# Output projection of the last four token tiles as three fp32r products, with half of W2 loaded later

## The reference, cut to what matters

```python
x = x + xattn(layernorm(x), ctx_1024, ...)   # 16 heads of 64; ends with: out @ Wo + bo, out is [1024, 1024], Wo is [1024, 256]
x = x + linear_attn(layernorm(x), ...)       # 16 heads of 16, causal within 64 tokens
x = x + ffn(layernorm(x), ...)               # top 2 of 8 experts; h = relu(x @ W1[e] + b1[e]); h @ W2[e] + b2[e]
```

## Time and profile before

| | |
|---|---|
| median of 3 runs | 1303.89 us (1302.39 to 1304.11) |
| profiled execution | 1302.54 us, span 1300.8 us |
| PE busy | 1272.9 us, 98% of the span |
| DVE, ACT, GpSimd busy | 75%, 47%, 47% |
| DMA, all queues | 145.56 MB, mean 112 GB/s |
| share of PE in the chain that ended last | 94% |

### The profile page before, as it was taken

How to read it: one execution, slowest core, us unless ns; L and a number is a source line. 1 busy time by engine, 2 the same in 40 slices (tenths; PEclk the granted TensorE clock), 3 DMA queues, 4 the chain that set the end, 5 groups by cost and what they waited for, 6 DMA issues and landing times.

```text
span 1300.8 us, 43872 instructions
## 1 busy us (share of the span) xinstructions
PE 1272.9 (98%) x18276; PEld 1135.4 (87%) x18276; DVE 979.4 (75%) x1970; ACT 616.1 (47%) x1250; POOL 608.3 (47%) x607
## 2 busy tenths in 40 slices
PE   7999999999999999999999999999999999999996
PEld 4589899889989988998998899899889888799996
DVE  7688777777877777877787788778766456768885
ACT  4344544444454444445444444544443333456663
POOL 3365455555445545545554555455443123333333
PEclk9999999999999999999999999999999999999998
DMA  6243443434343434343443435343444351566661
GB/s 218 59 108 89 111 100 89 119 75 107 89 111 75 115 87 107 75 121 83 103 115 86 107 75 121 80 107 82 117 108 112 102 198 35 184 188 182 194 196 47
DMA packets 71493, 145.56 MB, mean 112 GB/s; under 512 B 18232, under 2 KB 45568, under 8 KB 69120
## 3 DMA queue, kind: packets, MB, share of 16 engines
q1 hardware_dynamic: 67216, 138.53, 40.4%
q0 software_dynamic: 4080, 4.22, 1.6%
HBM read 61.74 MB, written 14.76 MB: 59 GB/s over the span
## 4 chain that ended last, share of the span: by engine, by line
PE 94%; DVE 2%; DMA 1%; issue 1%; POOL 1%; ACT 0%; SPq 0%; POOLq 0%; DVEq 0%; ACTq 0%
PE bank L1224 28%; PE bank L1256 9%; PE bank L1258 9%; PE bank L1257 9%; PE bank L1210 9%; PE bank L1514 6%; PE bank L1268 4%; PE bank L1240 2%; PE bank L1231 2%; PE bank L1345 2%; PE bank L1287 2%; PE bank L1561 2%; PE bank L1563 2%; PE bank L1562 2%; PE bank L1371 1%
## 5 line engine op out<-in xcount | busy, mean ns | idle before, releaser
L473 POOL TENSOR_TENSOR kr<-kr,ksw 128x1024 f32<-128x1024 f32 x128 | 318.4, 2488 | 458.3 <-DVE pr L814 350.3
L1256 PE MATMUL bank<-x_hi,p_hi 128*128 128x258 f32 x1024 | 300.9, 294 | 0.0
L1258 PE MATMUL bank<-x_hi,p_lo 128*128 128x258 f32 x1024 | 288.5, 282 | 0.0
L1257 PE MATMUL bank<-x_lo,p_hi 128*128 128x256 f32 x1024 | 287.8, 281 | 0.0
L1224 PE MATMUL bank<-ct_hi,wk_hi 128*128 128x512 f32 x512 | 214.3, 418 | 0.0
L829 DVE TENSOR_TENSOR kw<-bank,stab 128x1024 f32<-128x1024 f32 x128 | 156.7, 1225 | 63.9 <-PE bank L1224 63.9
L1224 PE MATMUL bank<-ct_hi,wk_lo 128*128 128x512 f32 x512 | 201.3, 393 | 0.0
L1224 PE MATMUL bank<-ct_lo,wk_hi 128*128 128x512 f32 x512 | 200.6, 392 | 0.0
L584 ACT COPY o_part<-bank 128x64 f32<-128x64 f32 x128 | 27.2, 213 | 363.6 <-PE bank L1268 363.6
L1257 PEld LDWEIGHTS bank<-x_lo,p_hi 128*128 128x128 f32 x1024 | 194.7, 190 | 0.0
L814 DVE TENSOR_SCALAR pr<-pr 128x1024 f32<-128x1024 f32 x128 | 89.0, 695 | 140.0 <-ACT pr L588 139.8
(11 more groups left out here) (206 smaller groups left out, 2169.8 us busy)
## 6 DMA issues: line engine op xcount, KB each, us to landing
ksw<-kw SPq DMA_DIRECT2D x512, 128.0 KB
raw<-in_ctx_dram SPq DMA_DIRECT2D x16, 1024.0 KB, 6.0
w_two<-in_L_ffn_W_dram SPq DMA_DIRECT2D x16, 1024.0 KB, 5.0
x_slots<-fill SPq DMA_DIRECT2D x128, 64.5 KB, 3.3
w_all<-in_L_ffn_W_dram SPq DMA_DIRECT2D x4, 2048.0 KB, 15.6
wo<-in_L_ffn_W_dram SPq DMA_DIRECT2D x7, 1024.0 KB, 4.9
xs<-x_slots SPq DMA_DIRECT2D x23, 129.0 KB, 2.1
raw<-in_x_dram SPq DMA_DIRECT2D x4, 512.0 KB, 4.3
```

The lines of the kernel that those rows point to most:

```text
L473: pool.tensor_tensor(kr[:, i], kr[:, i], ksw[:, i], ALU.add).then_inc(kr_done, 1)
L1256: pe.matmul(psZ[:, 0:D + 2], p_hi[:, i, c], x_hi[:, b, t], start=(t == 0), stop=False, skip_group_check=True)
L1257: pe.matmul(psZ[:, 0:D], p_hi[:, i, c], x_lo[:, b, t], start=False, stop=False, skip_group_check=True)
L1258: last = pe.matmul(psZ[:, 0:D + 2], p_lo[:, i, c], x_hi[:, b, t], start=False, stop=(t == ST - 1), skip_group_check=True)
```

## The change

The output projection of tiles 4 to 7 is computed with fp32r parts, 24 products instead of 8 fp32 ones for each tile. ACT makes the high parts: all of `wo` at the end of step 0 and one tile of `qo` at the end of each of steps 1 to 4. DVE makes the low parts: all of `wo` in step 1 and one tile of `qo` in each of steps 2 to 5, between `projected(s+1)` and `gating(s-2)`. PE's pairs 0 to 2 of these tiles wait for the low part of `qo`. The parts lie in the place of the second half of `w2_all`, so that experts 4 to 7 of W2 are loaded only when the last projection is done; in SP's list these two loads now stand behind `accumulate_from(5)`, and b2 stands behind `rows_in(2)`. The count of high parts (`EXPERT_PARTS` = 5) is added to the expert phase's waits.

```diff
-            for e in range(0, E, 2):
+            for e in range(0, E // 2, 2):
                 second_weights(e)
             for t in range(TT - 2):
                 accumulate_from(t)
             sp.wait_ge(y_ps, TT)
-            sp.dma_start(b2_all[:], b2.partition_broadcast(P)).then_inc(b2_ld, 16)
+            for e in range(E // 2, E, 2):
+                second_weights(e)
...
             for g in range(EARLY):
                 rows_in(g)
+            sp.dma_start(b2_all[:], b2.partition_broadcast(P)).then_inc(b2_ld, 16)
...
+            def output_weights_high():
+                act.wait_ge(z_ps, STEPS)
+                act.wait_ge(wo_ld, 32)
+                act.copy(wo_hi[:], wo[:]).then_inc(part_hi_done, 1)
+
+            def outputs_high(t):
+                if t >= FROM + 2:
+                    act.wait_ge(y_ps, t - 1)
+                act.copy(qo_hi[:, t % 2], qo[:, :, t * P:(t + 1) * P]).then_inc(part_hi_done, 1)
...
                 if s + 1 < TT:
                     turned(s + 1)
+                if s == 0:
+                    output_weights_high()
+                if FROM <= s + 3 < TT:
+                    outputs_high(s + 3)
...
+            def output_weights_low():
+                dve.wait_ge(part_hi_done, WO_PARTS + 1)
+                dve.tensor_tensor(wo_lo[:], wo[:], wo_hi[:].bitcast(F32), ALU.subtract).then_inc(part_lo_done, 1)
+
+            def outputs_low(t):
+                cols = slice(t * P, (t + 1) * P)
+                dve.wait_ge(part_hi_done, WO_PARTS + 1 + t - FROM + 1)
+                dve.tensor_tensor(qo_lo[:, :, cols], qo[:, :, cols], qo_hi[:, t % 2].bitcast(F32), ALU.subtract).then_inc(part_lo_done, 1)
...
                 if 2 <= s <= TT - 2:
                     projected(s + 1)
+                if s == 1:
+                    output_weights_low()
+                if FROM <= s + 2 < TT:
+                    outputs_low(s + 2)
                 if 0 <= s - 2:
                     gating(s - 2)
...
+                if first == 0 and t >= FROM:
+                    pe.wait_ge(part_lo_done, WO_PARTS + 1 + t - FROM + 1)
                 for g in range(first, end):
-                    last = pe.matmul(y_bank(t), qo[:, g, t * P:(t + 1) * P], wo[:, g], start=(g == 0), stop=(g == PAIRS - 1))
+                    cols = slice(t * P, (t + 1) * P)
+                    if t < FROM:
+                        last = pe.matmul(y_bank(t), qo[:, g, cols], wo[:, g], start=(g == 0), stop=(g == PAIRS - 1))
+                    else:
+                        pe.matmul(y_bank(t), qo_hi[:, t % 2, g], wo_hi[:, g], start=(g == 0), stop=False)
+                        pe.matmul(y_bank(t), qo_hi[:, t % 2, g], wo_lo[:, g], start=False, stop=False)
+                        last = pe.matmul(y_bank(t), qo_lo[:, g, cols], wo_hi[:, g], start=False, stop=(g == PAIRS - 1))
```

More of the change, by code:

```diff
@@ L55 @@
 WB, XB = 3, 3
+WO_PARTS = 0
+FROM = 4
+EXPERT_PARTS = WO_PARTS + 1 + TT - FROM
 def build(nc, x, ctx_1024, cos, sin, lat_g, lat_b, ctx_g, ctx_b, Wq, Wkv, Wo, bo, Wqkv, bqkv, Wout, bout, proj,
@@ L127, in build @@
         xl = raw[:, 1]
+        with ExitStack() as low:
+            qo_lo = sb("qo_lo", [P, PAIRS, TOK], F32R, low)
         qo = sb("qo", [P, PAIRS, TOK], F32, xattn)
@@ L194, in build @@
         result_no = sb("result_no", [P, 2], U32, lin)
+        with ExitStack() as middle:
+            sb("w2_first", [P, E // 2, FT, D], F32, middle)
+            wo_hi = sb("wo_hi", [P, PAIRS, D], F32R, middle)
+            wo_lo = sb("wo_lo", [P, PAIRS, D], F32R, middle)
+            qo_hi = sb("qo_hi", [P, 2, PAIRS, P], F32R, middle)
         w2_all = sb("w2_all", [P, E, FT, D], F32, lin)
@@ L261, in build @@
             sem(n) for n in ("z_ps", "rz_done", "zn_done", "zt_ps", "zts_done", "o_ps", "o_half", "o_done"))
-        w2_hi_done, w2_lo_done, h_split = sem("w2_hi_done"), sem("w2_lo_done"), sem("h_split")
+        part_hi_done, part_lo_done, h_split = sem("part_hi_done"), sem("part_lo_done"), sem("h_split")
         y_ps, y_done, bo_ld, x2_ld, xbo_done = (sem(n) for n in ("y_ps", "y_done", "bo_ld", "x2_ld", "xbo_done"))
@@ L725, in second_high @@
                     act.wait_ge(e_ps, g - 1)
-                act.copy(w2_hi[g % 2][:], w2_all[:, bass.ds(e, 1)].rearrange("p o f d -> p (o f) d")).then_inc(w2_hi_done, 1)
+                act.copy(w2_hi[g % 2][:], w2_all[:, bass.ds(e, 1)].rearrange("p o f d -> p (o f) d")).then_inc(part_hi_done, 1)
             act.wait_ge(group_done, 1)
@@ L1154, in second_low @@
                     dve.wait_ge(e_ps, g - 1)
-                dve.wait_ge(w2_hi_done, g - EARLY + 1)
+                dve.wait_ge(part_hi_done, EXPERT_PARTS + g - EARLY + 1)
                 dve.tensor_tensor(w2_lo[g % 2][:], w2_all[:, bass.ds(e, 1)].rearrange("p o f d -> p (o f) d"),
-                                  w2_hi[g % 2][:].bitcast(F32), ALU.subtract).then_inc(w2_lo_done, 1)
+                                  w2_hi[g % 2][:].bitcast(F32), ALU.subtract).then_inc(part_lo_done, 1)
             second_low(EARLY)
@@ L1556, in rows_out_parts @@
                     pe.wait_ge(ys_done, g)
-                    pe.wait_ge(w2_lo_done, g - EARLY + 1)
+                    pe.wait_ge(part_lo_done, EXPERT_PARTS + g - EARLY + 1)
                     pe.wait_ge(h_split, 4 * (g - EARLY + 1))
```

## The result

| | runs | median us | lowest to highest |
|---|---|---|---|
| kernel before | 10 | 1304.52 | 1302.39 to 1305.99 |
| changed kernel | 10 | 1309.05 | 1306.77 to 1310.03 |

The changed kernel takes 1.0032 times the time of the one before (95% interval 1.0023 to 1.0040), 4.5 us more. Its profiled execution took 1308.73 us (span 1307.0 us) against 1302.54 us: 6.2 us apart.

A forecast was written before the change was run, and what follows sets the result against it. PE (TensorE), 94% of the chain, was taken as the bound. A 5.0 us load wait (0.17 us saving inside) plus 2.2 us of clock gave 7.2 us, on the 1303.89 us median 1311.1, rounded 1311; 8-in-10 range 1306 to 1314.5 us.

The forecast's parts named there:

- the bound on DVE: Steps 2 to 5: `qo` subtractions delay the mask, leaving 0.13 us gain in each of 3 to 5; step 2 loses 0.45.
- the step from the profile to the median: Whole kernel: the 7.2 us priced on the profile was added to the median of 1303.89 us, giving 1311.1 us.
- Projection on PE: Output projection, tiles 4 to 7: three fp32r products save 0.077 us a pair, 0.61 us a tile, 2.5 us in all.
- The rule quoted from the Trainium skill: Projection's weight loads: 128 non-FP32 weights load by a faster path, saving PE up to about 1 us more; not counted.
- The worst case that I gave: Low parts of `qo` on DVE: 1.0 us later if the subtractions ran at L847's worst value.
- Low part of `wo`, ACT's casts: Step 1 on DVE: 2.29 us fits a 2.35 us wait, at most 0.1 us; ACT's casts fall in waits, nothing counted.
- The load behind W2: First expert rows: `xs` queues behind the late W2 loads, moving PE's L1462 by 5.0 us, bounds 3.5 to 8.4.
- The rival that small loads pass the large ones: At L1462: `xs` is served beside W2 and lands by 1124.6 us; total 1301.4 to 1303.7 us; chance 0.09.
- the one of a longer queue: SP's loads before the first rows: full queue holds issues or W2 needs 16 us, 2 to 3.4 us more; chance 0.14.
- The clock: After PE's wait for the first rows: clock falls to 0.50 for some 5 us, costing 2.2 us, between 0 and 2.8.
- The rival of a wait without the clock: After the first-rows wait: PE idles but its clock stays at 2.4 GHz, +5.0 us, 1308.9 us; chance 0.20.

The follow-up runs named there:

- e6: e1 with DVE's subtraction for each low part of `qo` done twice, the extra result unread: 1305.21 us, ratio 1.0004 to the kernel before.
- e9: Changed kernel with 17 unread fp32 products on PE ahead of the transpose of the first expert rows: 1304.33 us, ratio 1.0006 to the kernel before.
- e7: The kernel before, unchanged, run again for a second profile: 1303.96 us.
- e3: The kernel before with only the last W2 load (experts 6 and 7, 2 MB) moved late: 1304.76 us, ratio 0.9998.
- e1: Changed kernel with the parts in dead places and all W2 and b2 loads issued as in the kernel before: 1298.80 us, ratio 0.9959 to the latter.
- e10: e1 with 7 unread products on PE ahead of the last group's second layer: 1298.19 us, ratio 0.9955 to the kernel before.
- e11: e1 with 7 unread products ahead of the last group's second layer and two ahead of the first expert rows: 1296.74 us, ratio 0.9942 to the kernel before.
- e12: e1 again, unchanged, run beside e11: 1299.53 us, ratio 0.9965 to the kernel before.
- e4: Changed kernel with 12 unread fp32 products on PE ahead of the transpose of the first expert rows: 1305.68 us, ratio 1.0008 to the kernel before.
- e2: The kernel before with only SP's loads moved as in the changed kernel, projection still fp32: 1310.24 us, ratio 1.0049.
- e8: The kernel before with two unread products on PE ahead of the transpose of the first expert rows: 1302.26 us, ratio 0.9985.

## Why the prediction was right or wrong

Predicted 1311.0 us in 1306 to 1314.5 us, slower; measured 1309.05 us. Direction, place and mechanism held; one step, the bound on DVE, failed in its size, and so did the step from the profile to the median. By medians the change cost 4.5 us where I had said 7.2, and a kernel before that came out 0.6 us higher than the 1303.89 us I started from brought the forecast nearer: that 1311 lies only 2 us off is in part luck.

*Projection on PE: right.* A product costs 0.12 us (1099.51 to 1099.63 us above), and step 5 has 0.55 us less. The rule quoted from the Trainium skill, page "TensorE: Matmul & The Clock Gate", section "Weight-path perf modes — Fast Weight Load (FWL) and DoubleRow", doesn't show here either: the fp32r weight load of L1391 takes 188 ns, and the fp32 one of L1345 took 190 ns before.

*DVE becomes the bound: this step failed.* I had steps 3 to 5 gain 0.13 us each and step 2 lose 0.45 us. They gained 0.55 us each (12.61 to 12.06 us from start to start), and `weighted(2)` came 0.05 us late, the next `keys_queries` 0.25 us. I had written that the prediction is wrong if each of these steps shrinks by the whole 0.6 us; they come within 0.06 us of that. I took the reported end of a DVE instruction as the earliest start of the next. The rows show otherwise: L1104 starts 0.10 us after L912, which is reported with 0.18 us, and L967 starts 1.11 us after L1104, which is reported with 1.19 us. From L912's start to the gating I had 1.48 us and the trace has 1.21, and the mask starts 0.33 us after L920's start, not 0.41 us. Together that is 0.35 us of the 0.42 us by which I missed step 5. Some of it is my arithmetic: within the 1.48 us I added 1.30 us for a subtraction that I had priced at 1.26, and another 0.04 us comes from putting the mask 0.02 us late where my own terms make it 0.02 us early. The Trainium skill, page "Perfetto Trace Analysis", section "Summary: the profiler window per engine type", says that a DVE slice runs through the acknowledgement of its write; that agrees with starts that lie ahead of the reported end. So DVE is the bound, but by 0.07 us a step, and e6 shows how narrow that is: the next 1.10 us on DVE cost 1.12 us a step. The worst case that I gave, 1.0 us later with every subtraction at 2.49 us, was too small as well: four times the 1.27 us that each would take longer is 5.1 us.

*Low part of `wo`, ACT's casts: right.* L1099 fits in front of `residual(0)`, which starts at 16.73 us from step 0 (16.72 before), and nothing waits for ACT's casts.

*The load behind W2: right in kind, 0.2 us off in the sum, because two errors cancel; that is luck.* PE reached its end of the phase 1.64 us sooner, not 0.17, and so W2 was issued at 77.8 us from step 0, not at 79.3. But from there to the landing of `xs` it took 18.5 us (1110.10 to 1128.65), not 17.4: W2 took 15.7 us to land where my terms give 14.3, the rest 0.3 us less than I had. Sum: +4.8 us where I had +5.0. PE was ready that much sooner, so its wait was 7.36 us, not the 5 to 6 us that I had said would show it. Because the late loads are issued as soon as the middle phase gets there, the microseconds that PE saved did move them. The rival that small loads pass the large ones is out, since all four loads landed in the order of issue; the one of a longer queue holds for 1.1 us.

*The clock: right, 2.13 us against 2.2.* `weighted(7)` has 0.80 us of it and the hidden layer's first 16 instructions 1.15 us. e9 takes it away and gets 2.0 us back. The rival of a wait without the clock is out.

*From the profile to the median: wrong.* Step for step the profiled kernels are 6.9 us apart from step 0 to the end, where I said 7.2. The medians are 4.5 us apart. I added the whole 7.2 us to a median, as if a typical execution of before went like the profiled one. But e7 shows before with a clock that had fallen, which cost it 1.5 us, and the mean clocks say that a typical execution of before runs at the low clock for longer than the profiled one did: it pays some of what I charged to the change alone. e3 points the same way: its clock fell, and its median is that of the kernel before. In how many executions of before the clock falls at this place can't be told from two profiles.

*Open.* In the expert groups the kernels with the fp32 projection show two groups of 7.0 us among those of 6.66 us (0.7 us in all), PE's instructions being late without a named wait; the changed kernel, e1, e10 and e11 show none, e12, the same kernel as e1, one of 6.85 us, and e6 two of 6.86 us. No run tells why. Nor does any place in the profiles account for the whole of e1's 6.2 us by medians; 1.85 us (against the first profile) to 4.3 us (against e7's) are there at `rows_out(0)`. e1's five executions have a median mean clock of 0.997, the kernel before beside them 0.994, so part of the rest may lie in the clock; that isn't shown.

## What to carry to other kernels

Before a buffer is reused in a way that delays a load, ask what small, urgent load will be issued behind it in the same queue: here 4 MB moved late to make room for the parts cost 9 us at the first use of W2 in the profiles (5.3 and 10.7 us by medians), while the parts, laid in dead places, made the kernel 6.2 us faster by medians. Issuing the small load first was no way out, because the large one had a reader close behind. Where DVE is near the bound, take the time of an instruction from its start to the start of the next, not from its reported length. Where TensorE must wait, price the wait with the clock behind it, and if a wait can't be removed, fill it: with seven unread products at the end the last 24 took 1.5 to 2.2 us less. And where the kernel before has a wait on its path, take more than one profile of it: two of the same kernel differed here by 2.4 us at one place, and the mean granted clock of each execution can show whether the profiled one is typical.

## What the runs showed of the hardware

- Where PE waited 1.84 us (e7), 1.96 us (e4) and 2.02 us (e3), the clock fell to 0.50 behind the wait, and 16 instructions took 3.35 to 3.68 us in place of 2.05. Where it waited 7.36 us (changed kernel) and 7.18 us (e2) they took 3.20 and 3.79 us: the short waits cost these instructions as much as the long ones. Where it waited 0.90 us (before) and 1.07 us (e8) the clock stayed at 1.00.
- In e7 the clock still shows 1.00 up to 1126 us, and the wait had ended at 1124.65 us: the low clock appears only after the wait is over.
- Three times in step 5 a DVE instruction starts 0.08 us ahead of the reported end of the one before (L1104, L967, L942).
- A weight load of 128 x 128 took 188 ns in fp32r (L1391) and 190 ns in fp32 (L1345): no faster for fp32r.
- A 129 KB load issued behind 4 MB of W2 and 1 MB of W1 landed in 7.02 us in place of 2.96, and a scatter on GpSimd's own queue in 6.12 in place of 3.72: another queue is slowed as well, by 2.4 us.
